# Two heads of a pair in separate row halves of the query and key stacks of an attention stage

## The reference, cut to what matters

```python
q = (src @ Wq + bq).reshape(B, T, 16, 16)      # src = layernorm(x1)
k = (src @ Wk + bk).reshape(B, T, 16, 16)
v = (src @ Wv + bv).reshape(B, T, 16, 16)
scores = jnp.einsum('bqhd,bkhd->bhqk', q, k) * scale
probs = jax.nn.softmax(scores, axis=-1)
attn = jnp.einsum('bhqk,bkhd->bqhd', probs, v).reshape(B, T, 256) @ Wo + bo
```

## Time and profile before

| what | value |
|---|---|
| median of 3 runs | 735.25 us (731.07 to 739.47) |
| profiled execution: first to last instruction of the core | 734.8 us |
| mean granted TensorE clock in it | 0.852 of full |
| lead-in until the first matmul for maxima | 0 to 83.3 us |
| steps with scores, 128 of them | 111.7 to 481.6 us |
| routing and feed-forward part | 481.6 to 734.8 us |

### The profile page before, as it was taken

One profiled execution on the slowest core, in us unless ns is written; L12 is line 12 of the kernel. 1 busy time (PEld: TensorE's weight loads), 2 busy tenths in 40 slices (PEclk: granted clock), 3 DMA queues, 4 the chain that ended last, 5 costly groups with the idle time before them and its releaser, 6 DMA issues. The chain is left out here.

```text
span 734.8 us, 8824 instructions
## 1 busy us (share of the span) xinstructions
PE 538.7 (73%) x2528; PEld 347.9 (47%) x2528; DVE 452.3 (62%) x919; ACT 222.1 (30%) x405; POOL 216.0 (29%) x220
## 2 busy tenths in 40 slices
PE   2266498988998888998878988850267777788771
PEld 1232255444555345545333443220257777778771
DVE  5551477585776575776876666369846555555552
ACT  2002003453334343343444433681022222222220
POOL 4112201101010340010320003038046766667762
PEclk9997588898999887998988987995569888888885
DMA  5406520153020363020353164520001111111110
GB/s 136 122 0 207 162 63 30 58 171 94 15 72 3 116 188 87 2 72 1 134 146 55 44 146 144 186 73 29 0 24 34 52 41 45 29 46 41 50 43 15
DMA packets 41185, 54.69 MB, mean 74 GB/s; under 512 B 14207, under 2 KB 25471, under 8 KB 41152
## 3 DMA queue, kind: packets, MB, share of 16 engines
q1 hardware_dynamic: 35776, 38.32, 18.1%
q0 software_dynamic: 5376, 16.00, 7.1%
HBM read 37.25 MB, written 17.83 MB: 75 GB/s over the span
## 5 line engine op out<-in xcount | busy, mean ns | idle before, releaser
L630 DVE TENSOR_REDUCE mx<-amax 128x1 f32<-128x512 f32 x256 | 164.5, 684 | 77.2 <-PE amax L813 72.4
L505 ACT ACTIVATE probs<-sc 128x512 f32<-128x512 f32 x256 | 138.8, 595 | 194.7 <-PE sc L824 194.1
L813 PE MATMUL amax<-KS,QS 96*128 96x512 f32 x256 | 115.2, 500 | 54.5 <-DVE mx L630 29.8
L824 PE MATMUL sc<-QS,KS 100*128 100x512 f32 x256 | 110.9, 500 | 4.8 <-ACT probs L505 3.1
L813 PEld LDWEIGHTS amax<-KS,QS 96*128 96x128 f32 x256 | 49.7, 204 | 129.8 <-DVE mx L630 74.2
L380 POOL TENSOR_SCALAR var_eps<-mv 128x4 f32<-128x4 f32 x12 | 2.9, 241 | 285.7 <-DVE mv L537 284.7
L838 PE MATMUL pv<-probs,V 128*32 128x512 f32 x512 | 73.4, 699 | 0.0
L824 PEld LDWEIGHTS sc<-QS,KS 100*128 100x128 f32 x256 | 51.6, 206 | 40.1 <-ACT probs L505 21.4
L1175 PE MATMUL amax<-W_hi,hid_hi 128*128 128x256 f32 x160 | 54.0, 338 | 3.3 <-DVE hid_lo L1089 3.3
L1175 PE MATMUL amax<-W_hi,hid_lo 128*128 128x256 f32 x160 | 51.6, 322 | 0.0
L1175 PE MATMUL amax<-W_lo,hid_hi 128*128 128x256 f32 x160 | 51.3, 321 | 0.0
(11 more groups left out here) (180 smaller groups left out, 904.0 us busy)
## 6 DMA issues: line engine op xcount, KB each, us to landing
qk_dram<-HL SPq DMA_DIRECT2D x16, 512.0 KB, 3.0
QS<-qk_dram SPq DMA_DIRECT2D x96, 64.0 KB, 2.8
KS<-qk_dram SPq DMA_DIRECT2D x96, 64.0 KB, 2.8
W_sb<-in_L_ffn_W SPq DMA_DIRECT2D x4, 1024.0 KB, 6.7
xc<-in_x SPq DMA_DIRECT2D x4, 512.0 KB, 4.0
xc<-in_ctx SPq DMA_DIRECT2D x4, 512.0 KB, 5.1
x_dram<-xc POOLq DMA_DIRECT2D x4, 512.0 KB, 3.8
res_dram<-t_a POOLq DMA_DIRECT2D x4, 512.0 KB, 4.3
```

Of the source, the lines that this page charges most:

```text
L505: nc.scalar.activation(probs[:, n % 8, a * 512:(a + 1) * 512], sc[a][:, :], ACT.Exp, scale=SCALE).then_inc(exp_done, 1)
L630: nc.vector.reduce_max(mx[:, m % 16:m % 16 + 1], amax[m % 2][:, :], AX.X).then_inc(max_done, 1)
L813: nc.tensor.matmul(amax[m % 2][:, :], QS[0:96, pair, chunk * P:(chunk + 1) * P], KS[0:96, c, pair, :], start=True, stop=True).then_inc(A_f ...
L824: nc.tensor.matmul(sc[a][:, :], KS[0:100, c, pair, kc * P:(kc + 1) * P], QS[0:100, pair, :], start=True, stop=True).then_inc(sc_full, 1)
```

## The change

The stacks get a new layout. Head c = 0 lies in rows 0 to 47 and head c = 1 in rows 64 to 111 of both `QS` and `KS`. `KS` has one copy, no zero rows. The maxima lie behind each head (rows 48, 49 and 112, 113), and `KS` holds ones there. A score matmul reads one half: rows 0 to 49 or 64 to 113 (48 rows for the maxima). In a step n both heads of a pair are done for one block of 128 keys (before: one head, two blocks), and the order of TensorE's matmuls becomes score c = 0, maxima c = 1, score c = 1, maxima c = 0, and then the value round and the side task. One memset on GpSimd sets all of `KS` to 1.0; three on VectorE and one on GpSimd are gone. The number and size of stack transfers are the same.

```diff
-            KS = att("KS", [P, 2, H // 2, S], fp32r)
+            KS = att("KS", [P, H // 2, S], fp32r)
...
+        def maximum_of(m):
+            return m // 16 % G, m // 8 % 2, m // 2 % 4, 1 - m % 2
+        def rows_of(c, n):
+            return slice(64 * c, 64 * c + n)
...
-                        at = 48 * c + 16 * i
+                        at = 64 * c + 16 * i
...
-                for u in range(2):
-                    sp.dma_start(QS[96:100, 2 * g + u, :].bitcast(fp32),
-                                 m_dram[g % 2, :, :, :].rearrange("(h u c k) a i -> u c h (k a i)", h=2, u=2, c=2)[u]).then_inc(m_loaded[g % 2], 16)
+                for c in range(2):
+                    sp.dma_start(QS[64 * c + 48:64 * c + 50, 2 * g:2 * g + 2, :].bitcast(fp32),
+                                 m_dram[g % 2, :, :, :].rearrange("(h u c k) a i -> c h u (k a i)", h=2, u=2, c=2)[c]).then_inc(m_loaded[g % 2], 16)
...
-            nc.gpsimd.memset(KS[0:100, 0, :, :].bitcast(fp32), 0.0).then_inc(stack_ready, 1)
+            nc.gpsimd.memset(KS[:, :, :].bitcast(fp32), 1.0).then_inc(stack_ready, 1)
             pool.wait_ge(stack_ready, 1)
-            nc.gpsimd.memset(KS[96:98, 0, :, :].bitcast(fp32), 1.0).then_inc(stack_ready, 1)
-            pool.wait_ge(stack_ready, 2)
...
                 for m in (2 * n + 24, 2 * n + 25):
+                    g, u, chunk, c = maximum_of(m)
+                    at = 8 * u + 4 * c + chunk
                     dve.wait_ge(A_full, b * 64 + m + 1)
-                    nc.vector.reduce_max(mx[:, m % 16:m % 16 + 1], amax[m % 2][:, :], AX.X).then_inc(max_done, 1)
+                    nc.vector.reduce_max(mx[:, at:at + 1], amax[m % 2][:, :], AX.X).then_inc(max_done, 1)
...
-            nc.vector.memset(KS[0:48, 1, :, :].bitcast(fp32), 0.0).then_inc(ks_ready, 1)
...
-            nc.vector.memset(KS[96:100, 1, :, :].bitcast(fp32), 1.0).then_inc(ks_ready, 1)
...
-                    dve.wait_ge(ks_ready, 3)
-                    nc.vector.memset(KS[96:98, 1, :, :].bitcast(fp32), 0.0).then_inc(ks_ready, 1)
...
+            def score_for_maxima(b, m):
+                g, u, chunk, c = maximum_of(m)
+                if m % 16 == 0:
+                    pe.wait_ge(stack_loaded[g], (b + m // 64) * 192 + 192)
+                wait(pe, max_done, b * 64 + m - 1)
+                rows = rows_of(c, 48)
+                nc.tensor.matmul(amax[m % 2][:, :], QS[rows, 2 * g + u, chunk * P:(chunk + 1) * P], KS[rows, 2 * g + u, :], start=True, stop=True).then_inc(A_full, 1)
+            def score(b, n, c):
+                g, kc, u = n // 8 % G, n // 2 % 4, n % 2
+                if n % 8 == 0 and c == 0:
+                    pe.wait_ge(m_loaded[g % 2], (b + n // 32) * 64 + 32 * (g // 2 + 1))
+                pe.wait_ge(exp_done, b * 64 + 2 * n + c + 1)
+                rows = rows_of(c, 50)
+                nc.tensor.matmul(sc[c][:, :], KS[rows, 2 * g + u, kc * P:(kc + 1) * P], QS[rows, 2 * g + u, :], start=True, stop=True).then_inc(sc_full, 1)
...
-            def step(b, n):
-                scores(b, n)
+            def step(b, n, maxima):
+                for c in range(2):
+                    score(b, n, c)
+                    if maxima:
+                        score_for_maxima(b, 2 * n + 24 + c)
                 if n % 4 == 3 and not (isinstance(b, int) and b == 0 and n == 3):
                     weighted_values(b, n // 4 - 1)
...
                 for n in steps_of(part):
-                    step(b, n)
-                    if part != "last" or n < LAST_MAX:
-                        scores_for_maxima(b, n)
+                    step(b, n, part != "last" or n < LAST_MAX)
```

More of the change, by code:

```diff
@@ L321, in sp_program @@
                     store_qk(0, j)
-                sp.wait_ge(stack_ready, 2)
+                sp.wait_ge(stack_ready, 1)
                 load_stack(0, 0, side_of)
@@ L683, in dve_program @@
                 if task == ("gv", 0, 0):
-                    nc.vector.memset(V1[:, :, :, DH:2 * DH], 1.0).then_inc(ks_ready, 1)
-                    dve.wait_ge(ks_ready, 3)
-                    nc.vector.memset(KS[96:98, 1, :, :].bitcast(fp32), 0.0).then_inc(ks_ready, 1)
+                    nc.vector.memset(V1[:, :, :, DH:2 * DH], 1.0).then_inc(v1_ready, 1)
                 side_work(*task)
@@ L803, in side_work @@
                     tokens_out(bank, w_sb["Wo"], i, aT, O_full)
-            def scores_for_maxima(b, n):
-                for m in (2 * n + 24, 2 * n + 25):
-                    g, hh, chunk = m // 16 % G, m // 4 % 4, m % 4
-                    pair, c = pair_of(g, hh)
-                    if m % 16 == 0:
-                        pe.wait_ge(stack_loaded[g], (b + m // 64) * 192 + 192)
-                    wait(pe, max_done, b * 64 + m - 1)
-                    nc.tensor.matmul(amax[m % 2][:, :], QS[0:96, pair, chunk * P:(chunk + 1) * P], KS[0:96, c, pair, :], start=True, stop=True).then_inc(A_full, 1)
-            def scores(b, n):
-                g, r = n // 8 % G, n // 4
-                pair, c = pair_of(g, n % 4)
-                if n % 8 == 0:
+            def score_for_maxima(b, m):
[8 more added lines that the diff above has]
+                if n % 8 == 0 and c == 0:
                     pe.wait_ge(m_loaded[g % 2], (b + n // 32) * 64 + 32 * (g // 2 + 1))
-                for a in range(2):
-                    kc = 2 * (r % 2) + a
-                    pe.wait_ge(exp_done, b * 64 + 2 * n + a + 1)
-                    nc.tensor.matmul(sc[a][:, :], KS[0:100, c, pair, kc * P:(kc + 1) * P], QS[0:100, pair, :], start=True, stop=True).then_inc(sc_full, 1)
+                pe.wait_ge(exp_done, b * 64 + 2 * n + c + 1)
+                rows = rows_of(c, 50)
+                nc.tensor.matmul(sc[c][:, :], KS[rows, 2 * g + u, kc * P:(kc + 1) * P], QS[rows, 2 * g + u, :], start=True, stop=True).then_inc(sc_full, 1)
             def weighted_values(b, r):
@@ L838, in weighted_values @@
                         last = nc.tensor.matmul(pv[g % 2][32 * hh:32 * hh + 32, :], V1[:, kc, 8 * c + pair, :],
-                                                probs[:, (4 * r + hh) % 8, a * 512:(a + 1) * 512], start=(kc == 0), stop=(kc == TT - 1))
+                                                probs[:, (4 * r + 2 * a + hh // 2) % 8, c * 512:(c + 1) * 512], start=(kc == 0), stop=(kc == TT - 1))
                 last.then_inc(pv_round, 1)
-            def step(b, n):
-                scores(b, n)
+            def step(b, n, maxima):
[3 more added lines that the diff above has]
+                        score_for_maxima(b, 2 * n + 24 + c)
                 if n % 4 == 3 and not (isinstance(b, int) and b == 0 and n == 3):
@@ L853, in pe_program @@
                 side_work(*task)
-            pe.wait_ge(stack_ready, 2)
-            pe.wait_ge(ks_ready, 4)
+            pe.wait_ge(stack_ready, 1)
+            pe.wait_ge(v1_ready, 1)
             for n in range(-12, FIRST):
                 if n >= 0:
-                    step(0, n)
-                scores_for_maxima(0, n)
+                    step(0, n, True)
+                else:
+                    for m in (2 * n + 24, 2 * n + 25):
+                        score_for_maxima(0, m)
                 if n in LEAD_SIDE:
```

4 lines of the change are left out of this document (2 added, 2 removed).

## The result

The changed kernel takes 750.81 us (median of 4 runs, 749.85 to 752.13), the kernel before 737.36 us on the same chip (4 runs, 731.07 to 740.62). The ratio is 1.0211, 95% interval 1.0165 to 1.0257: 2% slower, above the predicted range and on the other side. Some runs of a kernel lie over 1.5% above its fastest run; the ratios leave them out, the medians have them in.

The account below looks back on a forecast made before the run. Plain steps were taken as bound by VectorE with a hole at each value round, projection steps by TensorE. Terms −13.9 − 9.4 + 5.2 + 3.4 = −14.7 took 735 to 720 us, range 706 to 744.

Parts of the forecast that it names:

- step 1: Value rounds moved behind the maxima matmuls: VectorE's reductions run beside the round, −13.9 us, between −7.8 and −29.
- step 6: Granted clock: two more value rounds at the lower clock because TensorE streams less of the time, +3.4 us.
- Step 2: Score and maxima matmuls of opposite row halves overlap, counting in 20 TensorE-bound steps: −9.4 us, up to +10.4.
- step 3: Two more changes of tile shape, 0.13 us each, in 20 TensorE-bound steps with a side task: +5.2 us, between 0 and +14.
- second rival: Plain stretches of third and fourth batch lose the full clock, 1.72 us more per value round: 744 us, chance 0.18.
- the gain is given back: VectorE catches up earlier, then waits for a projection, stack transfer or layer norm instead: about 735 us, chance 0.13.
- halves run one after another: Matmuls of opposite row halves don't overlap: 730 us, 740 with a stall at each switch; chance 0.22.
- Steps 4 and 5: Earlier waits for score and exp: 0, at most 0.1 us in 70 plain steps; fewer memsets: 0, at best −2.

Follow-up runs that it names:

- e9: Kernel before plus four unused matmuls into a free side bank in seven steps of a batch where TensorE waits for VectorE: 721.77 us beside 735.83, ratio 0.9816.
- e11: e7 with the unused matmuls of e9 placed behind the first score of the step: 715.55 us, ratio 0.9727.
- e4: Kernel before with scores read from rows 0 to 49 and maxima from rows 0 to 47 only, same order and matmul count: 810.33 us (one run) beside 737.51.
- e1: Kernel before with only the new matmul order (score, maxima, score, maxima, value round), full-row stacks kept: 736.56 us beside 737.51, ratio 1.0029.
- e7: Kernel before, full rows, with the new order in all steps but n = 15, 19 and 43: 735.97 us, ratio 0.9983.
- e8: Changed kernel (half rows) with the old order put back in steps n = 15, 19 and 43 alone: 761.62 us, ratio 1.0302.
- e6: Kernel before with score matmuls over all 128 rows instead of 100, added query rows zero, maxima left at 96: 733.52 us beside 738.04, ratio 0.9922.
- e2: Half-row stacks of the changed kernel in the order of the kernel before (both scores, value round, both maxima): 774.87 us beside 737.51.
- e10: Changed kernel with e9's idle-time matmuls over 128 rows, plus one ending each step without side task or value round in the two last batches: 733.73 us.
- e3: Changed kernel with each score matmul issued twice into the same bank: 771.81 us, ratio 1.0500.
- e5: Changed kernel with one unused 128-row matmul ahead of the first score of each step without a side task: 758.05 us, ratio 1.0279.

## Why the prediction was wrong

The forecast was 720 us, the kernel takes 750.81. Three terms of the sum missed: step 1 was −13.9 and came to nothing, step 6 was +3.4 and came to 14.1, and steps 2 and 3 were −4.2 together and came to −1.2.

*Step 6 failed, and with it the weight of the second rival.* The step counted two more value rounds at the lower clock, 1.72 us each. The traces have ten more: 18 rounds took over 2.7 us, 8 before. The value matmuls are busy for 14.1 us more, and the maxima matmuls take 575 ns instead of 500. In share of time, attention (the stretch with scores) has a granted clock of 0.79 over 380.1 us, from 0.89 over 370.3. With only the two levels that is an estimated 160 us at the lower one instead of 81.

The rival "the clock falls" had the place right (the plain stretches of the third and fourth batch, now 0.74 and 0.65), and its time of 744 us was nearest. That it came so near is partly luck: it set a debit of 27.5 against a gain of 18.1, and neither is what the runs have. It had 0.18, because of the earlier trace rows, three steps with scores alone at 1.00. The runs took that evidence away: with the same matmuls the last 12 steps ran at 1.00 before and at 0.74 and 0.71 in e9 and e11. One window at full clock said that it can be granted, not that it is safe. "Half rows may count for less than whole ones" stood in the prediction as half a sentence. e4 makes it the chief matter: with the number, columns and order of the matmuls as before, half the rows go with a clock lower by 0.09, and the kernel is 73 us slower, of which up to 21 are longer steps at the full clock.

The Trainium skill, TensorE: Matmul & The Clock Gate, Part 1, says that the clock is gated by how busy the array has lately been. The runs agree with it (idle time filled with unused matmuls: 0.852 to 0.879). How long the engine is busy is not the whole of it in e4: in 16 steps of the same matmuls over half the rows, with no more changes of shape, the clock is 0.65 instead of 0.83.

*Step 1, −13.9: right in the plain group, nothing in the sum.* e1 has 6.98 us where 6.69 was forecast and 7.44 before, so 0.46 of 0.75 a group, and the wait for maxima fell under 45 us as foretold (42.6). But e1 is not faster. The step took each hole as time won, and only plain groups at the full clock show it. Cut at the first score of each step, the 62 steps with maxima and without side task, in which 11.3 us were to be won, take 149.0 us before, 149.2 in e1 and 146.6 in the kernel after. Part of it goes to the clock even with full rows: 11 value rounds took over 2.7 us in e1, 8 before, which at 1.72 us each is an estimated 5 us. VectorE's three other waits grew by 13.4 us in e1 and 24.9 in the kernel after. The last rival, "the gain is given back", describes this and named the projection as the next wait. In e7 and e8 the three steps in which the round now stands behind a waiting maxima matmul were undone, and that brought nothing, so this is not where it is lost. e11 against e9 puts what remains of the gain at about 6 us with the idle time filled, with ranges that overlap.

*Step 2, −9.4, and step 3, +5.2: right in kind, wrong in size.* The pairs do start together. The term that was mis-sized is the time of two pairs: 0.67 us with the change of shape to the projection, predicted 0.47 + 0.13, because the second pair starts 0.35 us behind the first. A projection step gained 0.06 us, predicted 0.47 − 0.26 = 0.21; by 20 steps that is 1.2 us instead of 4.2. The change of shape to the projection cost about what was said: 0.32 from the second pair, of which a matmul is 0.21, so 0.11. The one back cost more, 1.92 − 1.71 = 0.21, so the two are 0.32 where 0.26 was predicted.

The Trainium skill, TensorEngine Tiling (Array Packing), Key Properties, holds that tiles work in parallel and that a new mode drains the engine. The trace agrees with both: starts within 0.01 us, and 0.11 and 0.21 us at the changes.

*The rival "halves run one after another"* is refuted by the same rows. *Steps 4 and 5*, waits and memsets at nothing: no row speaks against them. The first exp came at 115.6 us instead of 112.4, but in e1 and e7, which keep the memsets of before, it came at 115.7 and 112.0.

The sum with what was measured: order 0 (e1), overlap −1.2, clock +14.1, so 735 + 13 = 748 us, against a span of 748.3. The closeness is luck: the terms come from different runs, and the 14.1 us of the value matmuls are no measure of all that the clock costs. In e9 the clock rose and the batches got 20 us shorter while the value matmuls took as long as before (72.6 from 73.4 us).

**What stays open.** Whether the clock counts the rows in use or the height of the part of the array: after's matmuls have 48 of 64 rows in use, e4's on average 24 of 64 because of its zeros, and e6's zeros did no harm. A run with zeros up to row 63 of each half was not made. Nor is it separated in e4 how much of the lower clock comes from the rows and how much from the operands of zeros; the kernel after and e2 have no such zeros and lose clock too. Whether the halves cost anything with the idle time filled stays open (e10, whose runs lie 13 us apart).

## What to carry to other kernels

Ask of every edit to TensorE's work what it does to the granted clock, not only to its busy time: full-height matmuls with zero rows can be cheaper than half-height ones that overlap, and where other engines set the pace the overlap wins little anyway. Where TensorE waits on another engine and the windows show a clock under 1.00, put unused matmuls over many rows into that wait, outside of any other engine's chain (e9, e11: 2 to 3% won). Where such matmuls stood in the chain, e3 and e5, the kernel came out 3% and 1% slower than the one they were put into (ratios 1.0500 and 1.0279 beside 1.0211). Try an edit of the order only after that, since its gain can hide behind the clock.

## What the runs showed of the hardware that was not expected

- Matmuls over 48 to 50 rows instead of 96 to 100, with the same count and columns: granted clock 0.762 instead of 0.852, 810 us instead of 738 (one run; half of them with zeros in one operand). A projection step at the full clock took 3.04 us instead of 2.65.
- 96 unused matmuls in idle time: 736 to 722 us, with as many value rounds at the lower clock as before (8).
- Two matmuls in opposite row halves start within 0.01 us of each other, but the next pair starts 0.35 us later, where full-height matmuls follow each other every 0.235.
- The last 12 steps of attention, with the same instructions, took 18.04 us at 1.00 in the kernel before and 22.1 at 0.74 in e9, which differs only ahead of them.
